# The r gate of a GRU step on TensorE: low weight halves first, against the high half of h only

## The reference

```python
def cell(h, x):
    gi = x @ W_ih + b_ih
    gh = h @ W_hh + b_hh
    r = sigmoid(i_r + h_r); z = sigmoid(i_z + h_z)
    n = tanh(i_n + r * h_n)
    return (1.0 - z) * n + z * h
# experts
scores = einsum('btd,ed->bte', x, Wg); top 2; probs = softmax(top 2)
y += w_e * ((silu(x @ W1[e].T) * (x @ W2[e].T)) @ W3[e].T)
```

## Time and profile before

| What | us |
|---|---|
| Median of 3 runs | 1712.79 |
| The profiled execution | 1723.49 |
| Its span, first to last instruction | 1721.8 |
| First `gr_ps` matmul, last group's start | 44.96, 1488.1 |
| PE busy | 1459.1 (85%) |
| DVE busy | 1126.6 (65%) |
| ACT busy | 673.1 (39%) |
| POOL busy | 404.7 (24%) |

### The profile page before, as it was taken

The page is one execution under the profiler, slowest core; times in us unless marked ns, Lnnn a source line. Parts: engine busy times, 40 slices in busy tenths (PEclk is TensorE's granted clock), DMA queues, the critical chain, the costliest instruction groups (busy, mean ns, idle before and its releaser), DMA issues.

```text
span 1721.8 us, 69764 instructions
## 1 busy us (share of the span) xinstructions
PE 1459.1 (85%) x29785; PEld 1171.3 (68%) x29785; DVE 1126.6 (65%) x4419; ACT 673.1 (39%) x1564; POOL 404.7 (24%) x857
## 2 busy tenths in 40 slices
PE   4778675699999999999999999999999888766766
PEld 4666565677777777777777777777778676534433
DVE  5587676777777777777777777777777777612221
ACT  5354453333433343334333433343334333323333
POOL 1001221122222222222222222222222222232223
PEclk9788887699999999999999999999999988878888
DMA  8756464434444444444444444444444444557764
GB/s 273 230 167 179 122 156 124 170 119 128 159 137 137 137 162 137 137 137 142 127 125 138 150 139 133 124 136 137 137 137 137 137 137 137 165 190 239 226 216 151
DMA packets 93734, 265.71 MB, mean 154 GB/s; under 512 B 33007, under 2 KB 50415, under 8 KB 83312
## 3 DMA queue, kind: packets, MB, share of 16 engines
q1 hardware_dynamic: 75472, 227.60, 40.3%
q0 software_dynamic: 17952, 33.64, 8.7%
HBM read 217.47 MB, written 55.79 MB: 159 GB/s over the span
## 4 chain that ended last, share of the span: by engine, by line
PE 52%; DVE 24%; issue 7%; DMA 6%; ACT 5%; another core or an unknown queue 2%; POOL 2%; SPq 1%; DVEq 0%; POOLq 0%; ACTq 0%
PE gr_ps L1052 10%; PE gn_bank L1052 9%; PE b_ps L1073 8%; PE gz_ps L1052 6%; PE y_ps L1136 5%; PE b_ps L1099 4%; DVE hn L850 4%; DVE zpre L850 4%; PE gi_ps L1073 3%; PE a_ps L1099 3%; DMA work<-h_tok,mt 3%; DMA mt<-meta 3%; DVE hlog L882 2%; ACT zs L677 2%
## 5 line engine op out<-in xcount | busy, mean ns | idle before, releaser
L1052 PE MATMUL gr_ps<-hlog,whh 128*128 128x32 f16 x8192 | 249.7, 178 | 158.1 <-DVE hlog L885 137.5
L1052 PEld LDWEIGHTS gr_ps<-hlog,whh 128*128 128x128 f16 x8192 | 226.0, 96 | 230.3 <-DVE hlog L885 191.2
L1052 PE MATMUL gz_ps<-hlog,whh 128*128 128x32 f16 x8192 | 248.7, 178 | 6.1 <-issue 5.9
L1052 PE MATMUL gn_bank<-hlog,whh 128*128 128x32 f16 x8192 | 247.2, 177 | 6.0 <-issue 5.8
L535 POOL DMA_INDIRECT out_y<-work,mt x71 | 114.7, 1616 | 579.4 <-ACT work L721 400.5
L1052 PEld LDWEIGHTS gz_ps<-hlog,whh 128*128 128x128 f16 x8192 | 226.4, 97 | 7.6 <-issue 7.6
L1052 PEld LDWEIGHTS gn_bank<-hlog,whh 128*128 128x128 f16 x8192 | 225.5, 96 | 6.9 <-issue 6.7
L1073 PE MATMUL b_ps<-x_split,wih 128*128 128x512 f32 (+1 forms) x792 | 198.7, 396 | 0.3
L1136 PE MATMUL y_ps<-wbuf,work 128*128 128x512 f16 x639 | 176.7, 413 | 1.8 <-ACT work L698 1.8
L1099 PE MATMUL a_ps<-wbuf,work 128*128 128x352 f16 x852 | 151.2, 331 | 23.8 <-issue 23.8
L675 ACT ACTIVATE nt<-npre 128x64 f32<-128x64 f32 x256 | 65.7, 257 | 258.9 <-DVE npre L869 239.5
(11 more groups left out here) (159 smaller groups left out, 2135.5 us busy)
## 6 DMA issues: line engine op xcount, KB each, us to landing
wbuf<-wscr SPq DMA_DIRECT2D x71, 1410.0 KB
wbuf<-wscr SPq DMA_DIRECT2D x71, 768.0 KB
h_tok<-xrow SPq DMA_DIRECT2D x32, 256.0 KB
x_raw<-in_x_feat SPq DMA_DIRECT2D x7, 1024.0 KB, 6.1
wscr<-wbuf SPq DMA_DIRECT2D x9, 768.0 KB, 4.5
wscr<-wbuf SPq DMA_DIRECT2D x9, 706.0 KB, 4.2
wscr<-wbuf SPq DMA_DIRECT2D x9, 704.0 KB, 4.7
work<-in_w_units SPq DMA_DIRECT2D x8, 512.0 KB
```

The source lines that it names most:

```text
L1052: mm = pe.matmul(dst[:, j], whh[:, i, k, m * P:(m + 1) * P], h[:, k], start=(k == 0 and i == 0), stop=(k == K - 1 and i == 1))
```

## The change

`recur(t)` is cut in two for the r gate. First, after a wait for `H_HI` alone, 16 matmuls take the low weight halves against the high half of h: 16 columns each, into the first 16 columns of each block of `gr_ps`. Then TensorE waits for `H_LO`, and 16 matmuls take the high weight halves against both halves of h, 32 columns each. The product of the two low halves is left out for the r gate. [...] The gates n and z are as before.

```diff
             def recur(t):
+                h = h_parts(t - 1 if t else 2 * GS - 1)
+                if t:
+                    pe.wait_ge(gru_ops, gru(t - 1, "H_HI"))
+                for j in range(K):
+                    for k in range(K):
+                        pe.matmul(gr_ps[:, j, 0], whh[:, 1, k, j * P:(j + 1) * P], h[:, k, 0],
+                                  start=(j == 0 and k == 0), stop=False, skip_group_check=True)
                 if t:
                     pe.wait_ge(gru_ops, gru(t - 1, "H_LO"))
-                h = h_parts(t - 1 if t else 2 * GS - 1)
-                for dst, first in ((gr_ps, 0), (gn_ps, 2 * K), (gz_ps, K)):
+                for j in range(K):
+                    for k in range(K):
+                        mm = pe.matmul(gr_ps[:, j], whh[:, 0, k, j * P:(j + 1) * P], h[:, k],
+                                       start=False, stop=True, skip_group_check=True)
+                mm.then_inc(gh_ready, 1)
+                for dst, first in ((gn_ps, 2 * K), (gz_ps, K)):
                     for j in range(K):
                         m = first + j
                         for k in range(K):
```

## The result

| | us |
|---|---|
| Kernel before, median of 4 runs | 1711.51 (1709.28 to 1712.98) |
| Changed kernel, median of 4 runs | 1660.67 (1653.73 to 1664.51) |
| Ratio, 95% interval | 0.970 (0.967 to 0.973) |
| Predicted | 1682 (1668 to 1705) |

The kernel became 51 us faster, 3.0%. The experiments show that some 22 us are the gain that the prediction was about, and the other 29 us something that it had overlooked. The profiled executions lie further apart than the medians: their spans are 1721.8 and 1655.4 us.

The account below looks back on a forecast made before the run. The prediction took the GRU's loop through PE and DVE as the bound, with PE waiting for h's low half in some steps. Gains of 23 + 5 + 3 = 31 us from 1712.8 gave 1682 us, range 1668 to 1705.

Parts of the forecast that it names:

- Step 141: One of eight steps worked out: PE has 0.35 us of room, but DVE is busy until 866.75, so nothing is won.
- 1.50 us idle ahead of step 142: PE's idle time before step 142's r gate, read as waiting for h: the full 0.41 us counted as won.
- The eight steps: Steps 136 to 144: gains of 0.41, 0.41 and 0.26 us in steps 137, 142 and 143, together 1.08 us of 44.4.
- The early start itself: R gate ready up to 0.41 us earlier per waiting step: 3 us in early, 23 in middle, 5 in last steps.
- 16 columns at the pace of 32: In the r gate, 16-column matmuls take 25 ns each, as 32-column ones do, so PE-bound steps gain zero.
- The added wait costs nothing: One more wait per step in PE's queue, for the low half of h, was counted as zero.
- The bare load: Upper bound on the added wait: one weight load not hidden in every step, 0.05 us x 256 = 13 us.
- The idle time ahead of the r gate: Before the first r-gate matmuls, idle passes from L885 to L882 and sinks about 0.4 us per waiting step.
- (a): Rival: second half-gate starts late, or DVE queue, DMAs or POOL's lists become the limit; gain 15 us, 1698; chance 0.16.
- (b): Rival: the clock goes up as well; the range takes off 12 us more for it; chance 0.08.
- (c): Rival: clock falls more often in block matmuls of steps 48 to 255, 1.18 us a fall; 1737 us; chance 0.08.
- (d): Rival: no change, as POOL and the tiles set the loop and PE waits elsewhere; 1710 to 1713 us; chance 0.08.

Follow-up runs that it names:

- e7: Kernel before, with the z gate's signal put some 2.2 us later in 22 steps: 1714.65 us, ratio 1.025 to the kernel before.
- e8: Changed kernel, with the z gate's signal put later in 6 steps: 1660.15 us, ratio 0.992 to the kernel before.
- e9: Kernel before, unaltered, run again for its profile on a chip with almost no late signals: 1673.36 us.
- the calm pair: Unaltered kernel before (e9) and changed kernel (e10), on chips with almost no late signals: 1672.22 and 1650.41 us, ratio 0.986.
- e1: Changed kernel's new r-gate matmuls, but its first wait on the low half of h as before: 1678.28 us, ratio 1.003 to the kernel before.
- e10: Changed kernel, unaltered, run again on a chip with almost no late signals: 1650.41 us against 1672.22 us for the kernel before, ratio 0.986.
- e11: Kernel before with the new r-gate order only in the 32 steps t mod 8 = 5: 1687.24 us against 1716.65 us, ratio 0.984.
- e12: Kernel before with GpSimd's two indirect DMAs held until the z signal of steps t mod 8 = 5: 1684.88 us, ratio 0.981.

## Why the prediction was wrong, step by step

- **The step that failed** is "Step 141: ... the earlier r gate waits for DVE and the gain is lost". The earlier r gate does wait, at `R_A` (830.82, straight behind `base_e`, as forecast). But the prediction followed only the r gate. The z gate is earlier too, by 0.37 us against GpSimd, so that its signal was raised 0.10 us into GpSimd's DMA and not 0.47 us, and got through: VectorE's wait of 1.86 us went. The prediction said "No DMA and no other queue is touched" and did not ask how z then lies against GpSimd's queue. From r gate to r gate, step 141 took 872.33 - 865.38 = 6.95 us and then 834.33 - 829.06 = 5.27 us: 1.68 us where the prediction had nothing. By the difference between the kinds of chips, late signals cost about 39 us of the kernel before (1711.5 against 1672.2) and 10 us of the changed one (1660.7 against 1650.4): 29 us of gain that no term held. e7 and e8 give 42 and 10 us for delays put in by hand.
- **The row that should have shown it** stood in the prediction: 1.50 us idle ahead of step 142, which I took for the ordinary loop, where the others had 0.45 and 0.19 us. A hole three times as long as its neighbours, and there again at 515.90, asks where it comes from. The answer was further up the chain: `Z_A` 1.86 us late by "remote".
- **The eight steps.** Forecast 44.4 to 43.4 us. On the first chip 838.52 to 882.96 (44.44 us) became 803.63 to 844.69, 41.06 us. On the calm one 41.99 became 41.06 us, a gain of 0.93 against my 1.08: 0.35 at the start of step 137, 0.35 at that of step 141 (with no late signal TensorE sets the start of step 142: in e9 its r gate starts at 843.59, without idle time and 0.34 us after the low half of h, so the shift of 141 is kept), 0.23 at that of 143, none at 142. For a chip without late signals the sum was near, though two of its terms were wrong (nothing for 141, 0.41 for 142); that it came so near is luck. Of the 2.45 us between the kinds, 1.67 lie in step 141 and 0.72 in step 136, where the signal of the n gate came 0.73 us late.
- **The early start itself**: in the calm pair steps 0 to 48 gained 5.6 us, 48 to 224 16.5, the last 31 2.5 (298.4, 469.1 + 465.7, 162.1 us became 292.8, 460.5 + 457.8, 159.6). I had 3, 23 and 5. Together that is 24.6 us in these profiles and 22 us by the medians, so for a chip without late signals 31 was too much by 6 to 9 us, most of it in the middle steps.
- **16 columns at the pace of 32**: right. The 16 matmuls take 829.46 - 829.06 = 0.40 us.
- **The added wait costs nothing**: right. The four parts of recur stand without a hole (829.06, 829.46, 829.86, 830.66), and in e1, which has the added wait but no early start, the GRU takes 1393.5 us from the first r gate to the last, against 1395.2 in e9. The bare load that the prediction weighed at 13 us is not there.
- **The idle time ahead of the r gate**: right in kind; the 119 waits for L885 became 55 for L882. On the calm kind it was 102 and became 52, so the 17 others of the 119 belong to the first kind of chip, not to the loop that the prediction summed.
- **Rivals.** (a) VectorE, the DMAs and GpSimd did not take over: TensorE is busy for 98% of 600 to 800 us (195.37 of 200). (b) and (c) the clock, 0.925 and then 0.921, did not move the time. No run shows the 12 us that the range takes off for a better clock: in the calm pair, which gained 22 us, the granted clock went from 0.926 to 0.923 over the whole kernel and from 1.00 to 0.99 between 400 and 1300 us; in the first pair it rose from 0.99 to 1.00 between 400 and 1300 us and fell over the whole kernel. The 1.18 us a fall of (c) is 11.81 - 10.63 us. (d) is out by the 22 us of e10. None of them was the one that came true, a second effect on another queue.

## What to carry to other kernels

An idle time whose releaser the profile can't name is a term of its own: find it, and ask whether the change moves its two sides against each other, before summing what is left. When one engine's work moves by a few tenths of a us against another's, look at what the third engine does at that time; here TensorE's signal slipped in ahead of the point at which GpSimd's indirect DMA would have held it. And compare kernels within one job: the 40 us between jobs are nearly as much as this change brought, and the same change gained 51 us in one job and 22 in another.

## What the runs showed of the hardware

- A semaphore that TensorE raises 0.18 us or more after the start of a GpSimd indirect DMA (most of them 1.0 to 1.7 us long), and before its end, was late in 73 of 78, 32 of 39, 51 of 56 and 48 of 48 cases in four profiles from two jobs (before, after, e11, e12), by 0.1 to 2.4 us; within the first 0.18 us in 1 of 33. Elsewhere it was late in 4 of 593, 9 of 619, 7 of 601 and, with GpSimd's pair moved (e12), 29 of 621 cases. 40 of these 49 fall within 0.5 us behind the end of an indirect DMA, 21 of them r gates of e12, 0.2 us late; so the hold outlasts the DMA's record a little. Two indirect DMAs 0.3 us apart could hold it over both (2.37 us). ScalarE's signals got through at the same time: in step 141 `rh` started 0.52 us and `npre` 0.78 us after the start of the first indirect DMA in before, where TensorE's signal was late, and 0.52 and 0.79 us in e9, where it was not. TensorE itself ran on: its 12 matmuls into `b_ps`, behind the z gate, took 1.95 us in both.
- In eight profiles from three other jobs it was late in 5 of the 389 such cases whose signal the trace holds. What makes the difference between the two kinds (the chip, its firmware, another load on it) these runs can't say.
